# Turned copies, squares, values and distances on ScalarE, normalisation on GpSimd, and attention seams reordered, in a fused decoder layer on one core

## The chip, the core and the metric

The kernel runs on one core of a Trainium2 chip. The metric is the device time of one execution in microseconds; of the kernel before there are three runs, 987.98, 996.69 and 997.89 us, median 996.69 us. The engines are TensorE (PE, with its weight loads as PEld), VectorE (DVE), ScalarE (ACT), GpSimd (POOL) and SyncE (SP), which here only issues DMAs. Each engine takes its own instructions in order, and they wait for one another through semaphores.

## The reference, cut to what matters

The input x has 4 batches of 1024 rows of 256; the context has 4 x 77 rows of 256. All arithmetic is float32.

```
xn = layernorm(x)                                  # "x" normals
q, k, v = xn @ Wq / 4, xn @ Wk, xn @ Wv            # 16 heads of 16
A = (q k^T)^2, causal;  o = (A v) / (sum A + 1e-5) # per head
x1 = x + o @ Wo                                    # "wo"
s = layernorm(x1)                                  # "student" normals
D = sqrt(max(|ctx|^2 + |s|^2 - 2 ctx s^T, 0))      # 77 x 1024, "dist"
path = backtrack(dtw(D))                           # "warp": forward, backward
x2 = x1 + path^T @ ctx                             # "along"
y = layernorm(x2)                                  # "ffn" normals
out = x2 + gelu(y @ W1' + b') @ W2' + bias         # "hidden", "out"
```

W1' and W2' are W_exp and W_con multiplied by ten butterfly stages each; the kernel folds these once ("coef", "chain", "up", "mix", "w1", "down").

## The kernel before

One written list of units, `make_plan` (L94), sets the order of everything. Every engine's program loops over the same list (L567 GpSimd, L589 ScalarE, L775 VectorE, L988 TensorE, and the DMA queue of SyncE at L381) and does its part of each unit, so the relative order of all work on each engine is that of the list. `woven(parts, fill)` spreads a list of fill units evenly behind the parts.

- **Attention** of a batch is 48 steps (`attention_steps`): four groups of four heads, two halves of 512 query columns, key tiles of 128. A step n issues scores of n+1 on PE into `psS` (pair a, then b), products of n-1 into `psO`; ScalarE squares the scores into `A` (L609); GpSimd masks the diagonal tiles (L564); VectorE finishes a half (`heads_out`, L681). The first score of a batch waits for `s_stack`: the q and k parts are split into three bfloat16 pieces (L600 on ScalarE, L835 to L840 on VectorE), stored to HBM and read back stacked by twelve DMAs (`parts_out` L397, `stack_in` L404).
- **psW items.** All other matmul results go through the two banks of `psW` in turn. PE waits for `s_free` of the item two before; the reader waits for `s_ready`.
- **A layer norm** is `norm_units` (L68): four "stats" units of two 128x256 tiles (VectorE L800), "variance" (VectorE L805, L808, then ScalarE takes the root, L593), "rstd" (VectorE waits for the root, L811), four "normal" units of two tiles (VectorE L816), which write XN. Then four "turn" items: PE transposes four tiles into a bank (L1012) and VectorE copies it out (L825).
- **front(b)** is the norm of x, the turns, and eight "qk" items (PE L1021). **back(b)** is the student norm, then for each half of the 1024 columns two turns, whose squares ScalarE makes from the SBUF copy (L615), and one "dist" item: PE multiplies the context and the copy (L1049) and, after `s_sqt`, ones and the squares (L1052); VectorE adds and clips (L858), ScalarE takes the root (L623), SP stores (L418, L420). **values(b)** are four items (PE L1028, VectorE L844), **wo(b)** four (PE L1041, VectorE L853 adds to X).
- **Warps.** Two batches are warped together on VectorE: 104 forward rows (L730, L731, L733), whose distances SP reads back (L468), and 104 backward rows (L751, L752, L754). Each row depends on the one before. Warp 0 is woven with attention of batches 2 and 3, warp 1 with the feed-forward of batches 0 and 1. `ready(b)` adds along (L1102, L853), takes the ffn norm and turns; "hidden" is PE L1112 and a gelu on ScalarE (L655); "out" is PE L1122 and VectorE L940, L946.
- **Seams.** Behind the last steps of batch b the list has `values(b + 1) + both(b + 1) + wo(b)`, `both` being the first two scores. ready(0) is woven into the last four steps of batch 3, and back(3) into hidden(0, 0).
- **GpSimd's program** begins with constants, then for b = 1 to 3 waits for X of batch b-1 to land and issues the load of batch b (L537), then makes seven WIDEN tiles (L540); after that it enters the list.

## Time and profile before

| | |
|---|---|
| median of three runs | 996.69 us |
| the profiled execution, its own time | 998.89 us |
| its span, first to last instruction | 997.1 us |
| busy: PE, PEld | 795.2 us (80%), 385.3 us (39%) |
| busy: DVE, ACT, POOL | 603.5 us (61%), 405.9 us (41%), 124.6 us (12%) |
| mean granted TensorE clock | 0.883 |
| chain that ended last | DVE 33%, PE 25%, DMA 6% of the span |

Busy shares are means over stretches with different limits; the rows further down give them by stretch. PE lines are L966 (scores), L983 (products), L1028 (values), and so on as above. In a row of the trace, "xN" is a count, and the brackets at its end say how long the engine had been idle before it and what ended that. A timeline merges like instructions that follow each other on one engine. A granted clock of 1.00 is 2.4 GHz.

### The profile page before, as it was taken

The numbers are of one execution on the slowest core, as the hardware profiler recorded it, in microseconds if no ns is written. First come the engines' busy times: TensorE is split into PE (matmuls) and PEld (weight loads), VectorE is DVE, ScalarE is ACT, GpSimd is POOL, SyncE is SP. The second block draws the span as 40 slices with busy tenths as digits, with TensorE's granted clock in tenths as the row PEclk, the third lists the DMA queues.
The fourth block names the chain that finished last, engine by engine and source line by source line (L and its number), as shares of the span: only waits on it lengthen the run. The fifth ranks groups of instructions, "written<-read, shape, count | busy, mean of one in ns | idle before, by whom it ended". The sixth has DMA issues, their size and how long they took to land.

```text
span 997.1 us, 12566 instructions
## 1 busy us (share of the span) xinstructions
PE 795.2 (80%) x3919; PEld 385.3 (39%) x3919; DVE 603.5 (61%) x2611; ACT 405.9 (41%) x578; POOL 124.6 (12%) x306
## 2 busy tenths in 40 slices
PE   4889899998899897897777587796799342299998
PEld 2434234442234431233411122543575232256757
DVE  5743556433566427998599974646799888524002
ACT  1157874566673566652265555053013000032130
POOL 2123321132121122211121221000000000000000
PEclk9989899998799998898796798598799766599999
DMA  9785507665306753317505502001010001100001
GB/s 298 173 135 65 64 1 129 125 72 72 40 1 125 130 69 47 47 66 138 63 16 63 72 9 37 7 1 22 13 37 20 9 22 43 31 1 10 33 1 42
DMA packets 52133, 58.56 MB, mean 59 GB/s; under 512 B 22631, under 2 KB 31819, under 8 KB 52067
## 3 DMA queue, kind: packets, MB, share of 16 engines
q1 hardware_dynamic: 50979, 53.57, 31.5%
q0 software_dynamic: 1088, 4.19, 1.5%
q8 instruction: 31, 0.51, 0.2%
q14 instruction: 35, 0.29, 0.1%
HBM read 36.24 MB, written 21.50 MB: 58 GB/s over the span
## 4 chain that ended last, share of the span: by engine, by line
DVE 33%; PE 25%; DMA 6%; issue 3%; ACT 1%; SPq 1%; DVEq 0%; ACTq 0%
PE psS L1112 7%; PE psW L1122 6%; DVE FOLD L733 6%; DVE FOLD L754 6%; DVE FOLD L731 3%; DVE FOLD L752 3%; PE psW L1041 2%; DVE FOLD L730 2%; DVE FOLD L751 2%; DMA dist<-ARENA 2%; PE psS L966 2%; PE psW L1102 2%; PE psO L983 2%; DMA MORE<-dist 1%; DVE XX L816 1%
## 5 line engine op out<-in xcount | busy, mean ns | idle before, releaser
L609 ACT ACTIVATE ARENA<-psS 128x1024 f32<-128x1024 f32 (+3 forms) x384 | 295.1, 808 | 168.8 <-PE psS L966 165.7
L966 PE MATMUL psS<-ARENA 96*128 96x512 bf16 (+3 forms) x768 | 195.1, 351 | 62.5 <-ACT ARENA L609 54.9
L983 PE MATMUL psO<-ARENA 128*32 128x512 f32 (+3 forms) x1536 | 176.7, 535 | 1.5 <-POOL ARENA L564 1.5
L564 POOL TENSOR_SCALAR_AFFINE_SELECT ARENA<-ARENA 128x256 f32<-128x256 f32 x256 | 109.4, 433 | 469.7 <-ACT ARENA L609 466.9
L966 PEld LDWEIGHTS psS<-ARENA 96*128 96x128 bf16 x768 | 54.8, 101 | 250.1 <-ACT ARENA L609 180.5
L1122 PE MATMUL psW<-W2E,ARENA 128*128 128x256 f32 x512 | 116.2, 388 | 31.3 <-DVE ARENA L946 31.3
L1122 PEld LDWEIGHTS psW<-W2E,ARENA 128*128 128x128 f32 x512 | 99.3, 195 | 48.3 <-DVE ARENA L946 32.6
L655 ACT ACTIVATE ARENA<-psS,BEFF 128x512 f32<-128x512 f32 x64 | 43.4, 687 | 144.8 <-PE psS L1112 144.7
L1021 PE MATMUL psW<-XX,ARENA 128*128 128x512 f32 x128 | 63.3, 629 | 7.0 <-DVE XX L825 3.9
L1012 PE MATMUL psW<-IDENT,XX 128*128 128x128 f32 x192 | 34.8, 327 | 39.6 <-DVE XX L816 32.0
L754 DVE TENSOR_TENSOR_SCAN FOLD<-FOLD 64x37 bf16<-64x37 bf16 x208 | 61.8, 297 | 7.3
L733 DVE TENSOR_TENSOR_SCAN FOLD<-FOLD,MORE 64x37 f32<-64x37 f32 x208 | 60.8, 292 | 7.3
L853 DVE TENSOR_TENSOR X<-X,psW 128x512 f32<-128x512 f32 x32 | 21.9, 686 | 68.8 <-PE psW L1102 44.0
L593 ACT ACTIVATE SD<-VE 128x8 f32<-128x8 f32 x12 | 2.5, 206 | 141.8 <-DVE VE L808 141.8
L1112 PE MATMUL psS<-XX,MIXA 128*128 128x512 f32 x128 | 59.0, 607 | 0.0
L983 PEld LDWEIGHTS psO<-ARENA 128*32 128x32 f32 x1536 | 31.5, 112 | 69.1 <-issue 49.6
L1112 PE MATMUL psS<-ARENA,MIXA 128*128 128x512 f32 x128 | 55.3, 592 | 0.0
L730 DVE TENSOR_TENSOR FOLD<-FOLD 64x37 f32<-64x37 f32 x208 | 40.3, 194 | 15.5 <-DMA MORE<-dist 11.1
L1102 PE MATMUL psW<-CTX,ARENA 77*128 77x256 f32 x64 | 21.1, 486 | 34.0 <-DMA ARENA<-path 34.0
L1012 PEld LDWEIGHTS psW<-IDENT,XX 128*128 128x128 f32 x192 | 27.6, 169 | 50.2 <-issue 38.1
L1028 PE MATMUL psW<-ARENA,XX 128*128 128x256 f32 x128 | 35.2, 439 | 12.4 <-DVE ARENA L844 7.9
L751 DVE TENSOR_TENSOR FOLD<-FOLD 64x37 bf16<-64x37 bf16 x206 | 37.7, 183 | 5.8
(115 smaller groups left out, 793.1 us busy)
## 6 DMA issues: line engine op xcount, KB each, us to landing
ARENA<-qk_parts SPq DMA_DIRECT2D x192, 128.0 KB, 7.1
qk_parts<-ARENA SPq DMA_DIRECT2D x16, 768.0 KB, 4.3
out<-ARENA SPq DMA_DIRECT2D x16, 256.0 KB, 2.2
X<-in_x POOLq DMA_DIRECT2D x3, 1024.0 KB, 9.7
dist<-ARENA SPq DMA_DIRECT2D x4, 425.0 KB, 10.7
MORE<-dist SPq DMA_DIRECT2D x32, 52.6 KB
path<-MORE SPq DMA_DIRECT2D x52, 32.4 KB
dist<-ARENA SPq DMA_DIRECT2D x4, 300.5 KB
```

The costliest lines, as they stand in the source:

```text
L564: pool.affine_select(out=blk, in_=blk, compare_op=ALU.is_ge, fill=0.0, base=0, pattern=[[0, 2], [1, P]], channel_multiplier=-1).then_inc(s ...
L609: nc.scalar.activation(A[:, (2 * G + a) % A_PAIRS, :, 0:N], psS[:, a, :, 0:N], ACT.Square).then_inc(s_sq, 1)
L730: nc.vector.tensor_tensor(out=least, in0=above[:, 1:CB + 1], in1=above[:, 0:CB], op=ALU.min).then_inc(s_pre, 1)
L733: nc.vector.tensor_tensor_scan(row[:, 1:CB + 1], least, DSK[:, t // CH % 2, t % CH], row[:, 0:1], ALU.min, ALU.add).then_inc(s_row, 1)
L751: nc.vector.tensor_tensor(out=two, in0=below[:, 0:CB], in1=below[:, 1:CB + 1], op=ALU.add).then_inc(s_enter, 1)
L754: nc.vector.tensor_tensor_scan(row[:, 0:CB][:, ::-1], KIND[:, t][:, ::-1], two[:, ::-1], row[:, CB:CB + 1], ALU.subtract, ALU.is_lt).then_ ...
L966: ins = nc.tensor.matmul(psS[:, a, j, 0:N], KST[0:STACK, g % 2, 2 * a + j, kt * P:(kt + 1) * P], QST[0:STACK, g % 2, 2 * a + j, q0:q0 + N] ...
L983: ins = nc.tensor.matmul(psO[32 * j:32 * j + 32, o % 2, q0 - qc * HALF:q0 - qc * HALF + N], V1[:, kt, GH * g + j], A[:, (2 * G + j // 2) % ...
L1012: ins = nc.tensor.transpose(W[:, t * P:(t + 1) * P], XN[:, 4 * h + t, k * P:(k + 1) * P], IDENT[:])
L1021: ins = nc.tensor.matmul(W, WQKV[:, k, s * D + m * P:s * D + (m + 1) * P], XNT[:, k, h * HALF:(h + 1) * HALF], start=k == 0, stop=k == KD - 1)
L1112: ins = nc.tensor.matmul(psS[:, (n % 4) // 2, n % 2], W1E[:, k, m * P:(m + 1) * P], XFT[b % 2][:, k, h * HALF:(h + 1) * HALF], start=k == ...
L1122: ins = nc.tensor.matmul(W[:, j * D:(j + 1) * D], HGE[:, h, m, c:c + P], W2E[:, m, 0:D], start=m == 0, stop=m == HT - 1)
```

## The change

- The copies of "value", "turn_s" (student) and "turn_f" (ffn) items, and the add and clip of "dist", go from VectorE to ScalarE, which reads the PSUM bank itself; the squares of turned student tiles are made from PSUM too, and the bank is freed behind them. `s_sqt` goes; the "dist" matmuls wait for the turns' `s_free` alone. "turn_x" copies stay on VectorE.
- "normal" units go from VectorE to GpSimd. It waits for a new semaphore `s_rstd`, and for the last turn of the norm before.
- ScalarE's root becomes a unit of its own, "root", and empty "pause" units stand between variance, root and rstd.
- In the list, `both(b + 1)` comes before the last products of batch b and before values(b + 1) (in batch 0 too); wo(b) is woven into the statistics of back(b) of the next batch. back(3) and then ready(0) stand alone, in order, behind batch 3; warp 1 starts behind them, woven with both halves of hidden of batch 0.

```diff
@@ -65,13 +65,15 @@
...
 
-def norm_units(kind, b, before=()):
+def norm_units(kind, b, before=(), gap=0):
 
...
         stats = list(before[:2]) + sum(([s, u] for s, u in zip(stats, before[2:])), []) + stats[len(before) - 2:]
-    return stats + [("variance", kind, b), ("rstd", kind, b)] + [("normal", kind, b, i) for i in range(TT // 2)]
+    pause = [("pause",)] * gap
+    return (stats + [("variance", kind, b)] + pause + [("root", kind, b)] + pause + [("rstd", kind, b)]
+            + [("normal", kind, b, i) for i in range(TT // 2)])
 
...
@@ -94,11 +96,11 @@
...
     ns = len(attention_steps())
-    front = lambda b: norm_units("x", b) + [("turn_x", b, i) for i in range(4)] + [("qk", b, i) for i in range(8)]
-
-    def back(b, before=()):
+    front = lambda b, gap=2: norm_units("x", b, (), gap) + [("turn_x", b, i) for i in range(4)] + [("qk", b, i) for i in range(8)]
+
+    def back(b, gap=2):
         halves = [[("turn_s", b, 2 * h), ("turn_s", b, 2 * h + 1), ("dist", b, h)] for h in range(2)]
-        return norm_units("student", b, before) + sum(halves, [])
+        return norm_units("student", b, wo(b), gap) + sum(halves, [])
     values = lambda b: [("value", b, i) for i in range(TT // 2)]
...
@@ -120,27 +122,28 @@
...
 
-    plan = front(0) + [("w_exp", i) for i in range(4)] + values(0) + both(0)
+    plan = front(0, 0) + [("w_exp", i) for i in range(4)] + both(0) + values(0)
     for b, fill in ((0, [("context", i) for i in range(B)] + up + front(1)), (1, back(0) + down + front(2))):
         steps = steps_of(b)
-        plan += steps[0] + flat(woven(steps[1:-3], fill)) + flat(steps[-3:]) + values(b + 1) + both(b + 1) + wo(b)
+        plan += steps[0] + flat(woven(steps[1:-3], fill)) + flat(steps[-3:-1]) + both(b + 1) + steps[-1] + values(b + 1)
 
     steps = steps_of(2)
-    third = woven(steps[:LEAD], back(1)) + woven(steps[LEAD:-3], front(3)) + steps[-3:] + [values(3) + both(3) + wo(2)]
+    third = (woven(steps[:LEAD], back(1, 1)) + woven(steps[LEAD:-2], front(3)) + [steps[-2] + both(3)] + steps[-1:]
+             + singles(values(3)))
     steps = steps_of(3)
     fourth = woven(steps[:-LAST], back(2))
-    plan += flat(third[:LEAD + SLACK]) + flat(woven(third[LEAD + SLACK:] + fourth, warp(0))) + paths(0)
-    plan += flat(steps[-LAST:-4]) + flat(woven(steps[-4:], ready(0)))
-
-    plan += wo(3)[:2] + flat(woven(singles(back(3, wo(3))[2:]), hidden(0, 0)))
-    rest = [hidden(0, 1), ready(1), outs(0, 0) + outs(0, 1), hidden(1, 0) + hidden(1, 1), outs(1, 0) + outs(1, 1)]
-    pieces = woven(singles(rest[0]), rest[1]) + singles(rest[2] + rest[3] + rest[4])
+    plan += flat(third[:LEAD + SLACK]) + flat(woven(third[LEAD + SLACK:] + fourth, warp(0))) + paths(0) + flat(steps[-LAST:])
+
+    plan += back(3, 0) + ready(0)
+    rest = [hidden(0, 0) + hidden(0, 1), ready(1), outs(0, 0) + outs(0, 1), hidden(1, 0) + hidden(1, 1), outs(1, 0) + outs(1, 1)]
+    pieces = singles(rest[0][:HT]) + woven(singles(rest[0][HT:]), rest[1]) + singles(rest[2] + rest[3] + rest[4])
     plan += flat(woven(pieces, warp(1), [4 if piece[0][0] == "out" else 1 for piece in pieces])) + paths(1) + ready(2)
...
 
+ON_SCALAR = ("qk", "value", "turn_s", "turn_f", "dist")
 ITEM_KINDS = ("context", "w_exp", "turn_x", "qk", "value", "wo", "turn_s", "dist", "coef", "chain", "up", "w1", "down", "along", "turn_f", "out")
...
@@ -568,6 +572,15 @@
...
                     mask(*u[1:])
+                elif kind == "normal":
+                    _, what, b, i = u
+                    if i == 0:
+                        pool.wait_ge(s_rstd, norm_of[what, b] + 1)
+                        if norm_of[what, b]:
+                            pool.wait_ge(s_ready, ready(*turned[norm_of[what, b] - 1]))
+                    for t in (2 * i, 2 * i + 1):
+                        ins = pool.tensor_scalar(XN[:, t], X[:, b, t], MV[:, t, 0:1], RS[:, t:t + 1], ALU.subtract, ALU.mult)
+                    ins.then_inc(s_xn, 1)
                 elif kind == "coef" and u[1] == 1:
...
@@ -588,7 +601,7 @@
...
                 kind = u[0]
-                if kind == "variance":
+                if kind == "root":
                     act.wait_ge(s_var, norm_of[u[1:]] + 1)
...
@@ -607,19 +620,36 @@
...
                     nc.scalar.activation(A[:, (2 * G + a) % A_PAIRS, :, 0:N], psS[:, a, :, 0:N], ACT.Square).then_inc(s_sq, 1)
+                elif kind == "value":
+                    _, b, i = u
+                    act.wait_ge(s_ready, ready(*u))
+                    for j in range(2):
+                        ins = nc.scalar.activation(V1[:, 2 * i + j, :, 0:HD],
+                                                   psW[:, bank(*u), j * D:(j + 1) * D].rearrange("p (h e) -> p h e", h=NH), ACT.Copy)
+                    ins.then_inc(s_free[bank(*u)], 1)
                 elif kind == "turn_s":
...
                     h, k = i // 2, i % 2
-                    act.wait_ge(s_free[bank(*u)], made(*u))
+                    if i == 0 and b + 1 < B:
+                        act.wait_ge(s_parts_out, 64 * (b + 2))
+                    act.wait_ge(s_ready, ready(*u))
                     SNT, SQT = BACK[b][0:2]
-                    nc.scalar.activation(SQT[:, k, h * HALF:(h + 1) * HALF], SNT[:, k, h * HALF:(h + 1) * HALF],
-                                         ACT.Square).then_inc(s_sqt, 1)
+                    nc.scalar.activation(SNT[:, k, h * HALF:(h + 1) * HALF], psW[:, bank(*u)], ACT.Copy)
+                    nc.scalar.activation(SQT[:, k, h * HALF:(h + 1) * HALF], psW[:, bank(*u)], ACT.Square).then_inc(s_free[bank(*u)], 1)
+                elif kind == "turn_f":
+                    _, b, i = u
+                    h, k = i // 2, i % 2
+                    act.wait_ge(s_ready, ready(*u))
+                    nc.scalar.activation(XFT[b % 2][:, k, h * HALF:(h + 1) * HALF], psW[:, bank(*u)], ACT.Copy).then_inc(s_free[bank(*u)], 1)
                 elif kind == "dist":
...
                         act.wait_ge(s_dist_out[B - 2], 32)
+                    act.wait_ge(s_ready, ready(*u))
+                    DSQ, DN = BACK[b][2:4]
+                    nc.scalar.activation(DSQ[0:S, h * HALF:(h + 1) * HALF], psW[0:S, bank(*u)], ACT.Relu, bias=AA[:, b:b + 1]
+                                         ).then_inc(s_free[bank(*u)], 1)
                     act.wait_ge(s_free[bank(*u)], made(*u))
-                    DSQ, DN = BACK[b][2:4]
                     nc.scalar.activation(DN[0:S, h * HALF:(h + 1) * HALF], DSQ[0:S, h * HALF:(h + 1) * HALF],
...
@@ -801,6 +831,8 @@
...
                     settled()
+                    if norm_of[u[1:]]:
+                        dve.wait_ge(s_xn, TT // 2 * norm_of[u[1:]])
                     for t in range(TT):
...
@@ -808,21 +840,13 @@
...
                     dve.wait_ge(s_sd, norm_of[u[1:]] + 1)
-                    vec(nc.vector.reciprocal(RS[:], SD[:]))
-                    settled()
-                elif kind == "normal":
-                    _, what, b, i = u
-                    for t in (2 * i, 2 * i + 1):
-                        ins = nc.vector.tensor_scalar(XN[:, t], X[:, b, t], MV[:, t, 0:1], RS[:, t:t + 1],
-                                                      ALU.subtract, ALU.mult)
-                    ins.then_inc(s_xn, 1)
-                elif kind in ("turn_x", "turn_s", "turn_f"):
+                    nc.vector.reciprocal(RS[:], SD[:]).then_inc(s_rstd, 1)
+                elif kind == "turn_x":
                     _, b, i = u
                     h, k = i // 2, i % 2
-                    if kind == "turn_s" and i == 0 and b + 1 < B:
-                        dve.wait_ge(s_parts_out, 64 * (b + 2))
-                    dst = {"turn_x": XNT, "turn_s": BACK[b][0], "turn_f": XFT[b % 2]}[kind]
-                    nc.vector.tensor_copy(dst[:, k, h * HALF:(h + 1) * HALF], got).then_inc(freed, 1)
+                    if b and i == 0:
+                        dve.wait_ge(s_ready, ready("value", b - 1, TT // 2 - 1))
+                    nc.vector.tensor_copy(XNT[:, k, h * HALF:(h + 1) * HALF], got).then_inc(freed, 1)
                 elif kind == "qk":
...
@@ -852,11 +870,6 @@
...
                                             op=ALU.add).then_inc(freed, 1)
-                elif kind == "dist":
-                    _, b, h = u
-                    DSQ = BACK[b][2]
-                    nc.vector.tensor_scalar(DSQ[0:S, h * HALF:(h + 1) * HALF], got[0:S], AA[:, b:b + 1], 0.0,
-                                            ALU.add, ALU.max).then_inc(freed, 1)
                 elif kind == "w1":
```

## Rows read from the trace of the kernel before

**Rows 1.** Windows of five stretches: busy us (count), granted clock, DMA share, GB/s.

```profile
186.00:317.00 131.00, 117.76 (x695) 41.79 (x694) 65.31 (x158) 87.74 (x133) 28.72 (x71) 0.92 0.41 59
384.00:612.00 228.00, 170.10 (x966) 59.27 (x970) 192.77 (x1023) 111.91 (x155) 40.72 (x94) 0.83 0.36 56
612.00:684.00 72.00, 63.09 (x245) 33.20 (x238) 31.19 (x86) 29.64 (x39) 3.25 (x8) 0.86 0.16 19
...
719.00:856.00 137.00, 78.76 (x287) 55.36 (x285) 123.53 (x782) 12.28 (x17) 0.00 (x0) 0.80 0.08 25
856.00:997.00 141.00, 126.78 (x448) 85.57 (x448) 33.63 (x78) 26.03 (x37) 0.00 (x0) 0.92 0.07 20
```

**Rows 2.** Timeline of POOL, first 42 us: start, duration, operation, idle before.

```profile
27.30 0.88 POOL L537 DMA_DIRECT2D X<-in_x  x1 [9.10 <-DMA X<-in_x]
28.18 2.48 POOL L540 COPY FOLD<-IDENT 64x128 f32<-64x128 f32 x7
```

**Rows 3.** Timeline of DVE over the first 42 us.

```profile
10.50 2.67 DVE L816 TENSOR_SCALAR XX<-X,MV,RS 128x256 f32<-128x256 f32 x8
```

**Rows 4.** Timeline of PE over the first 75 us.

```profile
18.14 17.93 PE L1021 MATMUL psW<-XX,ARENA 128*128 128x512 f32 x32 [2.27 <-DMA WOP<-in_L_attn_Wo]
...
41.72 8.27 PE L1028 MATMUL psW<-ARENA,XX 128*128 128x256 f32 x32
53.69 1.41 PE L966 MATMUL psS<-ARENA 96*128 96x512 bf16 x4 [3.70 <-DMA ARENA<-qk_parts]
```

**Rows 5.** Timeline of the SP queue over the first 75 us.

```profile
38.43 11.11 SPq L411 DMA_DIRECT2D ARENA<-qk_parts  x24
```

**Rows 6.** Timeline from 300 to 345 us, the seam of batches 1 and 2.

```profile
304.76 0.60 ACT L600 ACTIVATE ARENA<-psW 128x512 bf16<-128x512 f32 x1 [0.69 <-PE psW L1021]
...
315.93 0.64 PE L983 MATMUL psO<-ARENA 128*32 128x256 f32 x8
...
317.40 7.25 PE L1028 MATMUL psW<-ARENA,XX 128*128 128x256 f32 x32
...
326.41 1.06 PE L966 MATMUL psS<-ARENA 96*128 96x512 bf16 x4 [1.76 <-DMA ARENA<-qk_parts]
...
327.28 8.76 PE L1041 MATMUL psW<-WOP,ARENA 128*128 128x256 f32 x32
```

**Rows 7.** Groups of DVE, 384 to 612 us: busy, mean ns, idle before, releaser.

```profile
L754 DVE TENSOR_TENSOR_SCAN FOLD<-FOLD 64x37 bf16<-64x37 bf16 x104 | 32.0, 308 | 3.7
...
L816 DVE TENSOR_SCALAR XX<-X,MV,RS 128x256 f32<-128x256 f32 x16 | 5.8, 400 | 0.0
...
L844 DVE COPY ARENA<-psW 128x256 f32<-128x256 f32 x8 | 2.9, 409 | 4.5 <-PE psW L1028 4.5
...
L853 DVE TENSOR_TENSOR X<-X,psW 128x512 f32<-128x512 f32 x4 | 2.7, 686 | 5.0 <-PE psW L1041 5.0
...
L825 DVE COPY ARENA<-psW 128x512 f32<-128x512 f32 x4 | 2.7, 664 | 0.8 <-PE psW L1012 0.8
...
L858 DVE TENSOR_SCALAR ARENA<-psW,AA 77x512 f32<-77x512 f32 x2 | 1.5, 748 | 7.0 <-PE psW L1052 7.0
```

**Rows 8.** Groups of POOL from 384 to 612 us.

```profile
L564 POOL TENSOR_SCALAR_AFFINE_SELECT ARENA<-ARENA 128x256 f32<-128x256 f32 x94 | 40.7, 439 | 178.1 <-ACT ARENA L609 176.9
```

**Rows 9.** Groups of DVE from 719 to 856 us.

```profile
L754 DVE TENSOR_TENSOR_SCAN FOLD<-FOLD 64x37 bf16<-64x37 bf16 x104 | 29.7, 286 | 3.7
```

**Rows 10.** The chain that ended last, by time: start, us, what.

```profile
661.49 1.72 PE psW L1049 x4
...
674.55 7.16 DMA dist<-ARENA
```

**Rows 11.** Timeline of DVE from 682 to 722 us.

```profile
684.13 0.19 DVE L730 TENSOR_TENSOR FOLD<-FOLD 64x37 f32<-64x37 f32 x1 [5.19 <-DMA MORE<-dist]
...
697.57 0.17 DVE L811 RECIPROCAL RS<-SD 128x8 f32<-128x8 f32 x1
...
718.66 2.29 DVE L940 TENSOR_TENSOR ARENA<-X,BIAS 128x2048 f32<-128x2048 f32 x1 [4.78 <-PE psW L1122]
```

More of the change, by code:

```diff
@@ L160, in layer @@
     item_of = {u: k for k, u in enumerate(u for u in plan if u[0] in ITEM_KINDS)}
+    turned = [u for u in plan if u[0] in ("turn_x", "turn_s", "turn_f") and u[2] == 3]
     norm_of = {u[1:3]: k for k, u in enumerate(u for u in plan if u[0] == "variance")}
@@ L309, in layer @@
         s_sd = sem("s_sd")
+        s_rstd = sem("s_rstd")
         s_xn = sem("s_xn")
```

10 lines of the change are left out of this document (1 added, 9 removed).

## The prediction

> **What bounds the kernel now.** I read the windows first, then the chain of waits and the engine timelines at each joint, then the groups of VectorE. The span has four kinds of stretch. Up to the first score at 53.69 us everything is serial: statistics, normalisation, turning, q and k, a round trip of q/k parts through HBM, scores [rows 3 to 5]. Then three attention batches run near TensorE's limit: 117.8 of 131 us busy, at a granted clock of 0.92 [rows 1]. From 384 to 612 us the first warp is woven in and VectorE bounds: 192.8 of 228 us busy against 170.1 on PE and 111.9 on ACT, and what is missing is mostly VectorE waiting inside its own order (7.0 us for distances, 5.0 for wo, 4.5 for values) [rows 1, 7]. From 719 to 856 us VectorE's second warp bounds alone (123.5 of 137 us), and from 856 us PE does (126.8 of 141) [rows 1]. So an instruction taken off VectorE is worth its length in two stretches and nothing where PE bounds; and a step moved in the serial head costs all its delay.
>
> **Start: normals go behind GpSimd's loads.** Now the normals of batch 0 begin at 10.50 us on DVE [rows 3]. In the new program they stand in GpSimd's order after its three loads of X, each issued only when the one before has landed, and after the seven WIDEN copies: the last issue is at 27.30 us, the copies end at 30.66 [rows 2]. Nothing in the diff moves these. The wait is 30.66 - 10.50 = 20.2 us. No row shows a tensor_scalar on GpSimd. Nearest is its affine_select of the same 128x256 tile, 439 ns [rows 8]; below it zero is the end, above it the WIDEN copies, 2.48/7 = 0.35 us for half as many columns, so 0.71 us [rows 2]. I take 0.44: eight make 3.5 us against DVE's 2.67, +0.8. Of this, 1.5 us is forgiven, since the q matmuls wait 2.27 us for weights now [rows 4]. The last X load overlapped the first stores of q/k and no longer does, my estimate is -3 us (0 to -4). The first score comes 16.5 us later, near 70 us. Second, the values: 8.27 us of PE at 41.72, done today under the wait for the stacked parts (which take from 38.43 to 53.69) [rows 4, 5]. The new plan puts them after the first scores, in the open: +8.3, less 1.8 for squares that now lie beside them. **Start: +23** (17 to 29).
>
> **Two seams, 0 to 1 and 1 to 2.** The fourth q/k piece is ready at 304.76 us, the stack has landed at 326.41: 21.6 us. The last-but-one products end at 316.57, and the values fill 317.40 to 324.65, so PE waits 1.76 us only [rows 6]. The new order asks for the next batch's first scores right after the last-but-one products. The pieces before it are the same, so PE stands from 316.6 to 326.4, and then does last products (0.4) and values (7.25). Step 1 starts at about 326.4 + 1.1 + 0.6 + 7.3 + 1.5 (slower clock after a stop, an estimate: the first 128x256 values at 41.72 took 8.27 against 7.25 here) = 336.9, against 336.0 today (327.28 + 8.76) [rows 4, 6]. Today wo lies inside that time, in the new plan its 32 matmuls, of the shape of the values, 7.3 us, are still to come, woven into steps where PE is already 90% busy [rows 1]. I take 5 of them as not hidden (0 to 7.3). **Seams: 2 x 6 = +12** (-4 to +17). ScalarE takes the values here: eight copies, shorter than the 0.60 us of a 128x512 one [rows 6], beside 7.25 us of PE: nothing; their cover is gone only if ScalarE becomes full. The third seam costs nothing: VectorE is behind there.
>
> **384 to 612 us.** Off VectorE go 16 normals (5.8 us), 8 value copies (2.9), 4 turned copies (2.7), 2 distances (1.5): 12.9 us. With them go the waits in which it stood for the distance matmuls (7.0), values (4.5), turns (0.8), and, as wo is spread, 4 of 5.0 [rows 7]: 16.3 us. GpSimd costs something back: the warp's scan takes 308 ns here and 286 where GpSimd rests [rows 7, 9], 2.3 us over 104; with the warp's three like instructions some 7 us beside 40.7 us of GpSimd [rows 8]; 16 normals add 7 us of it, so +1.2 to 2. Next late are the DMAs of distance rows and ACT: it gets 8 value copies, 4 turned copies at 0.60 and 2 relus, 8 us on 111.9 of 228 [rows 1, 6], covered. The pauses let VectorE reach rstd after the root is done, and ACT the root after the variance. Pool's masks queue behind normals that wait for rstd; products wait for masks, but PE is ahead of VectorE. **-27** (-10 to -32).
>
> **612 to 719 us.** Today 72.1 us pass from the end of warp 0 to the first row of warp 1, 684.13 [rows 1, 11], with ready(0) and half of the hidden layer before it. New: rest of attention 12 us, wo 7, last add, statistics and variance 4, root, rstd and four normals 2, then two turns, four ScalarE passes (0.60 each [rows 6]), two pairs of distance matmuls (2 x 1.72 each [rows 10]), relu and root, for two halves: 17; the store and first load of distances as today, 674.19 to 684.13, 10 [rows 10, 11]. That is 52, and ready(0) fits under the DMA. Warp 1 starts 20 us earlier. Normals and turned copies of ready(1) also leave VectorE (-5), but it now reaches the first out product, 21 us behind rstd today (697.57 to 718.66), with more wait than today's 4.78 us, about 8, because 16 hidden tiles come later (+3), and four pieces done before 684 fall behind the start (+3) [rows 11]. **-19** (-9 to -23). The cover of the new order is the DMA's 10 us; without it ready(0) would be in the open.
>
> **Tail.** ready(2) and ready(3) gain 8 and 4 normals on the way, 0.1 us each, and copies that queue behind gelus: **+1** (0 to +4) on the 141 us [rows 1]. That ScalarE squares from PSUM rather than SBUF I cost at nothing; it was busy beside the same matmuls before.
>
> Sum: 23 + 12 - 27 - 19 + 1 = **-10 us**, from the profiled 998.89 (span 997.1) to 989. That execution lies 2.2 above the median of 996.69, and its changes are taken over: 987; I say **988**.
>
> **A rule against the change.** GpSimd's same-sized select takes 439 ns and DVE's normal 400 [rows 7, 8], hardly different. The Trainium skill, GPSIMD Engine Reference, section 4.1, calls GpSimd about 2x slower than VectorE for two-input elementwise work, though one-input is "roughly line-rate". By the first half of it a normal would take 0.8 us, and as 28 of them lie on the path the sum would be 998; by that page's second half it stays 988.
>
> **Rivals.** (a) *The seams are free*: the stack lands earlier, since its contending store is later, and wo hides under squares: seams -2 instead of +12, warp stretch at its full 30: 971. For it: ACT has 43 us free in 186 to 317 [rows 1]; against: 21.6 us from the fourth piece is a chain of two DMAs [rows 6]. Chance 0.25. (b) *GpSimd's normals are dear*, the case on the other side: some 28 normals stand alone in a chain (8 at the start, 4 in back(3), 4 in ready(1), 12 in the tail), plus the blocked warp instructions, 30 us of time per us of normal. It decides slower than before from (997 - 988)/30 + 0.44 = 0.74 us each, and over 1% slower from 1.06; at 1.2 us the time is 1011. For it: 0.35 us for half a tile in WIDEN; against: 439 ns [rows 2, 8]. Chance 0.18. (c) *Another engine holds the 384 to 612 stretch*: GpSimd waits for rstd, masks wait, PE (170.1 of 228 busy) catches up too late, and only 10 of 27 us come: 1005. For it: PE's granted 0.83 [rows 1]; against: VectorE has no wait for products there. Chance 0.17. My forecast 0.40. That the copies don't move isn't possible; the code names the engine.
>
> **Numbers.** What a measurement of this kernel can tell from no change is 1%, 986.7 to 1006.7. My forecast itself spans 978 to 999 and gives 0.17 faster, 0.23 same; (a) 0.23 and 0.02; (b) 0.15 slower, 0.03 same; (c) 0.10 same, 0.07 slower. Together 0.40, 0.38, 0.22. Range 965 to 1012: it leaves out the far ends of (a) and (b).
>
> **What would show it.** In the profile after: first normal on GpSimd at 30.7 us and first score near 70; a PE wait of 7 to 10 us for the stacked parts at both seams; the warp stretch about 200 us long with no DVE wait for distances; first row of warp 1 about 52 us after warp 0; normals of 0.4 to 0.5 us. Wrong if normals start before 25 us, if they take over 0.8, or if the first stretch's loss is given back in batch 0.

## The result and the profile after

| kernel | median, us | runs, us | against before |
|---|---|---|---|
| before | 996.71 | 987.98 to 997.89 | |
| changed | 1043.26 | 1041.46 to 1046.35 | 1.049 [1.0426, 1.0555] |

The changed kernel is 4.9% slower. The forecast was 988 us with a range to 1012, so sign and range are both missed. The profiled execution of the changed kernel took 1041.46 us (span 1039.7).

The groups of the changed kernel's page, by cost (columns as in [rows 7]):

```profile
L568 POOL TENSOR_SCALAR_AFFINE_SELECT ARENA<-ARENA 128x256 f32<-128x256 f32 x256 | 107.7, 427 | 415.7 <-ACT ARENA L622 413.2
L582 POOL TENSOR_SCALAR XX<-X,MV,RS 128x256 f32<-128x256 f32 x96 | 118.1, 1241 | 257.5 <-DVE RS L843 257.5
L1025 PE MATMUL psW<-IDENT,XX 128*128 128x128 f32 x192 | 38.1, 350 | 96.1 <-POOL XX L582 93.7
L979 PE MATMUL psS<-ARENA 96*128 96x512 bf16 (+3 forms) x768 | 193.7, 348 | 59.0 <-DMA ARENA<-qk_parts 35.9
```

One number stands out. A normal takes 1241 ns on GpSimd. The forecast took 440, from the select in the first row, which is still as quick as in [rows 8]. TensorE's turns stand idle for 93.7 us in all behind those normals, against 38.0 us behind VectorE's in kernel a below. The last row is the seams: 35.9 us of waiting for stacked parts.

The start, on POOL and then on PE (start us, duration, operation, idle before), answers to [rows 2 to 4]:

```profile
26.90 0.88 POOL L541 DMA_DIRECT2D X<-in_x  x1 [8.27 <-DMA X<-in_x]
27.77 1.69 POOL L544 COPY FOLD<-IDENT 64x128 f32<-64x128 f32 x7
29.47 9.64 POOL L582 TENSOR_SCALAR XX<-X,MV,RS 128x256 f32<-128x256 f32 x8
```

```profile
34.45 1.94 PE L1025 MATMUL psW<-IDENT,XX 128*128 128x128 f32 x8 [34.45 <-POOL XX L582]
39.26 1.94 PE L1025 MATMUL psW<-IDENT,XX 128*128 128x128 f32 x8 [2.87 <-POOL XX L582]
42.03 17.64 PE L1034 MATMUL psW<-XX,ARENA 128*128 128x512 f32 x32 [0.83 <-issue]
73.91 1.89 PE L979 MATMUL psS<-ARENA 96*128 96x512 bf16 x4 [8.42 <-DMA ARENA<-qk_parts]
```

The queue is as forecast: loads, WIDEN, then normals at 29.47 us. But eight of them last 9.64 us and not 3.5, and the first score comes at 73.91 us, 20.2 later than in [rows 4].

The seam of batches 1 and 2 (from the last products of one batch to the first scores of the next) in the changed kernel, PE, answers to [rows 6]:

```profile
370.01 0.64 PE L996 MATMUL psO<-ARENA 128*32 128x256 f32 x8
380.61 1.89 PE L979 MATMUL psS<-ARENA 96*128 96x512 bf16 x4 [9.96 <-DMA ARENA<-qk_parts]
383.01 8.27 PE L1041 MATMUL psW<-ARENA,XX 128*128 128x256 f32 x32
```

The scores are asked for before the values, so PE stands for 9.96 us. Before, the values filled that time and left 1.76. At the seam of batches 0 and 1 it is 7.61 us, so both lie in the 7 to 10 that the forecast named.

To see where time is lost I read the same events in each trace: the first scores of each batch, the last products, and the first and last row of warp 1. This table gives the length between them, to about half a microsecond, since a row is taken by its start. Kernels j, a, o and c are experiments below; j copies where the others normalise, so its results are not those of the layer.

| stretch, us | before | changed | j: 0.4 us copies in place of the normals, GpSimd | a: normals on VectorE | o: half of them | c: best |
|---|---|---|---|---|---|---|
| to first score | 53.7 | 73.9 | 65.7 | 51.3 | 53.6 | 53.4 |
| batch 0 | 122.8 | 137.4 | 129.9 | 132.6 | 137.8 | 124.9 |
| batch 1 | 150.0 | 169.3 | 157.3 | 155.9 | 168.7 | 148.3 |
| batch 2 | 159.2 | 156.1 | 152.6 | 152.8 | 158.0 | 146.1 |
| batch 3 | 146.4 | 122.8 | 121.4 | 121.3 | 124.1 | 118.9 |
| to first row of warp 1 | 52.2 | 42.4 | 39.3 | 40.0 | 39.7 | 39.8 |
| warp 1 | 170.0 | 181.2 | 169.7 | 171.4 | 171.5 | 171.5 |
| from its last row to the end | 142.9 | 156.6 | 144.7 | 144.6 | 143.9 | 144.5 |
| span | 997.1 | 1039.7 | 980.6 | 969.8 | 997.2 | 947.3 |

### The profile page after: what moved, and what is told of

The parts are those of the page before. It is cut to its first block, busy times and chain, and to the rows that moved or that the text cites. A ratio compares the mean times of both kernels' runs of the same rounds, so it can differ in the third digit from the quotient of the medians.

```text
span 1039.7 us, 12584 instructions
## 1 busy us (share of the span) xinstructions
PE 794.4 (76%) x3919; PEld 385.5 (37%) x3919; DVE 537.2 (52%) x2443; ACT 431.0 (41%) x644; POOL 239.6 (23%) x402
## 4 chain that ended last, share of the span: by engine, by line
PE 39%; DVE 27%; POOL 8%; issue 8%; DMA 8%; ACT 6%; SPq 2%; POOLq 0%; DVEq 0%; ACTq 0%
POOL XX L582 7%; PE psS L979 7%; PE psO L996 7%; PE psW L1134 6%; DVE FOLD L784 5%; PE psS L1124 5%; DVE FOLD L763 4%; DMA ARENA<-qk_parts 4%; ACT ARENA L622 3%; PE psW L1041 2%; DMA X<-in_x 2%; DVE FOLD L782 2%; DVE FOLD L761 2%; PE psW L1054 2%; PE psW L1034 2%
## 5 line engine op out<-in xcount | busy, mean ns | idle before, releaser
L979 PE MATMUL psS<-ARENA 96*128 96x512 bf16 (+3 forms) x768 | 193.7, 348 | 59.0 <-DMA ARENA<-qk_parts 35.9
L996 PE MATMUL psO<-ARENA 128*32 128x512 f32 (+3 forms) x1536 | 174.4, 528 | 15.3 <-POOL ARENA L568 14.9
L582 POOL TENSOR_SCALAR XX<-X,MV,RS 128x256 f32<-128x256 f32 x96 | 118.1, 1241 | 257.5 <-DVE RS L843 257.5
L1134 PE MATMUL psW<-W2E,ARENA 128*128 128x256 f32 x512 | 114.6, 385 | 20.5 <-DVE ARENA L959 20.2
L1025 PE MATMUL psW<-IDENT,XX 128*128 128x128 f32 x192 | 38.1, 350 | 96.1 <-POOL XX L582 93.7
L1025 PEld LDWEIGHTS psW<-IDENT,XX 128*128 128x128 f32 x192 | 30.2, 184 | 109.0 <-issue 105.1
L718 DVE STREAM_TRANSPOSE ARENA<-psO 128x512 f32<-128x512 f32 x32 | 22.5, 704 | 77.9 <-PE psO L996 77.8
L1124 PE MATMUL psS<-XX,MIXA 128*128 128x512 f32 x128 | 62.2, 640 | 0.0
L1124 PE MATMUL psS<-ARENA,MIXA 128*128 128x512 f32 x128 | 55.3, 592 | 0.0
L613 ACT ACTIVATE ARENA<-psW 128x512 bf16<-128x512 f32 x32 | 19.1, 597 | 75.6 <-PE psW L1034 75.6
L760 DVE TENSOR_TENSOR FOLD<-FOLD 64x37 f32<-64x37 f32 x208 | 42.7, 206 | 7.7 <-DMA MORE<-dist 2.5
## 6 DMA issues: line engine op xcount, KB each, us to landing
dist<-ARENA SPq DMA_DIRECT2D x4, 425.0 KB, 10.5
```

Source lines behind the costliest of these rows:

```text
L582: ins = pool.tensor_scalar(XN[:, t], X[:, b, t], MV[:, t, 0:1], RS[:, t:t + 1], ALU.subtract, ALU.mult)
L979: ins = nc.tensor.matmul(psS[:, a, j, 0:N], KST[0:STACK, g % 2, 2 * a + j, kt * P:(kt + 1) * P], QST[0:STACK, g % 2, 2 * a + j, q0:q0 + N] ...
L996: ins = nc.tensor.matmul(psO[32 * j:32 * j + 32, o % 2, q0 - qc * HALF:q0 - qc * HALF + N], V1[:, kt, GH * g + j], A[:, (2 * G + j // 2) % ...
L1025: ins = nc.tensor.transpose(W[:, t * P:(t + 1) * P], XN[:, 4 * h + t, k * P:(k + 1) * P], IDENT[:])
L1124: ins = nc.tensor.matmul(psS[:, (n % 4) // 2, n % 2], W1E[:, k, m * P:(m + 1) * P], XFT[b % 2][:, k, h * HALF:(h + 1) * HALF], start=k == ...
L1134: ins = nc.tensor.matmul(W[:, j * D:(j + 1) * D], HGE[:, h, m, c:c + P], W2E[:, m, 0:D], start=m == 0, stop=m == HT - 1)
```

## The experiments

Each was timed beside the kernel before on the same chip. The experiments lie on four chips, on which the kernel before had medians of 995.5 to 998.5 us, so a difference of 2 or 3 us between kernels of two chips may be the chip's. My theory after the result (G) was that GpSimd's price of a normal costs nearly all; the rivals were the new order at the seams (S) and VectorE's stretch taking back what is given (C).

### a: all normals on VectorE

```
-                elif kind == "normal":                       # GpSimd
-                        ins = pool.tensor_scalar(XN[:, t], ...)
+                elif kind == "normal":                       # VectorE, waits s_rstd
+                        ins = nc.vector.tensor_scalar(XN[:, t], ...)
```

> The changed kernel with all 96 normals back on VectorE; the plan, the ScalarE part and the seams stay as changed. Theory G (the normals on GpSimd are what makes the changed kernel slow: 1241 ns each there instead of 400 on VectorE, 8 of them behind the X loads in the start): first score back from 73.9 to about 53 us, the 8 normals of a chain back from 9.6 to 3.4 us, so 980 to 1000 us, 43 to 60 below the changed kernel. Theory S (the new order at the seams and in the start is what costs): no more than 25 us come back, 1018 us or more. Theory C (VectorE then holds the stretch of warp 0 as in the kernel before, and what the start gives back is lost there): about 1005 us, with the stretch of warp 0 some 15 us longer than in the changed kernel.

Measured: 970.89 us (969.9 to 971.6), 0.9743 [0.9702, 0.9784] of before. 72 us come back, more than G expected; S and C are out as the main cause (c shows below that the order costs too). Without its GpSimd part the change is a gain of 2.6%. Against the changed kernel the table gives 22.6 us in the start, 18.2 in batches 0 and 1, 4.8 in batches 2 and 3, 2.4 to the first row, 9.8 in warp 1, 12.0 in the tail: 69.8 of 69.9.

### e: only the normals moved

```
 (kernel before)
-                        ins = nc.vector.tensor_scalar(XN[:, t], ...)
+                        ins = pool.tensor_scalar(XN[:, t], ...)
```

> The kernel before with nothing changed but the engine of the 96 normals, which is GpSimd. Theory G: about 1240 ns each, the start 20 us later, 6 us more in each of the chains that PE waits for (student 3, ffn 0 to 3) and masks held back in batches 0 and 1: 1035 to 1055 us. Theory S: the normals cost only the start, 1010 to 1018 us.

Measured: 1045.57 us, 1.0504 [1.0451, 1.0557]. As G expected. This one move alone costs 47 us (1045.6 - 998.5), as much as the whole change. It costs more still in the new order, 72 us by a. Against before, the profiled execution of e loses 20.3 us in the start, 12.5 in batches 0 and 1, 8.2 on the way to warp 1 and 13.0 in the tail. In the new order batches 0 and 1 lose 18.2 and warp 1 another 9.8, where e loses nothing. Why the new order feels the normals more there, no run sets apart.

### d: only the ScalarE part, in the order of before

```
 (changed kernel, normals on VectorE)
-    make_plan() as changed
+    make_plan() as before, "root" put between "variance" and "rstd"
```

> The kernel before, its order of work as it was, with only the ScalarE part of the change: value copies, copies and squares of turned tiles, and distances read from PSUM on ScalarE; the normals stay on VectorE. Theory G: VectorE loses about 31 us of copies (32 turns and 32 value pairs and 8 distances) while it holds the stretch of warp 0, so 975 to 990 us. Rival (ScalarE, which squares every pair of scores, holds batches 0 to 2 when it copies too, and PE's values wait for it): 997 to 1005 us, with PE waiting for psW behind ScalarE at each values block.

Measured: 978.69 us, 0.9822 [0.9771, 0.9873]. As G expected. Warp 0 lasts 211.9 us instead of 229.2. ScalarE hardly holds anything: PE's waits for it before scores are 29.1 us in all, against 54.9 before, and new are 10.1 us before the distance matmuls, which now wait for ScalarE's copies.

### f: what makes a normal dear

```
+            pool.wait_ge(s_ready, ready("turn_f", 3, 3))
+            for r in range(3):
+                pool.tensor_scalar(XN[:, 0], X[:, 3, 0], MV[:, 0, 0:1], RS[:, 0:1], ALU.subtract, ALU.mult)
+                pool.tensor_scalar(XN[:, 1], X[:, 3, 1], 0.5, 2.0, ALU.subtract, ALU.mult)
+                pool.tensor_scalar(XN[:, 2], X[:, 3, 2], MV[:, 2, 0:1], None, ALU.subtract)
+                pool.tensor_scalar(XN[:, 3], X[:, 3, 3], 0.5, None, ALU.subtract)
+                pool.tensor_copy(XN[:, 4], X[:, 3, 4])
+                pool.tensor_tensor(out=XN[:, 5], in0=X[:, 3, 5], in1=X[:, 2, 5], op=ALU.mult)
+                pool.tensor_scalar(XN[:, 6:8], X[:, 3, 6:8], MV[:, 6, 0:1], RS[:, 6:7], ...)
```

> The first of these kernels (normals on VectorE) with 21 extra GpSimd instructions once the last tiles are turned, in three rounds, on unused space, 128x256 each: the normal as it is (two values per partition), the same with two constants, a subtraction alone with a value per partition, the same with a constant, a copy, a product of two tensors, and one normal over 128x512. Theory 1 (the two per-partition values make it dear): 1.2 us for the first and about 0.4 to 0.5 us for those with constants or one operation. Theory 2 (GpSimd takes that long for any fp32 tile of this size, each operation adding): copy and one operation about 0.6 us, two operations about 1.2 us whatever their scalars. Theory 3 (it is fixed cost): the 128x512 one takes hardly more than the 128x256 one.

One run (975.13 us). Groups of POOL from 900 us on, where the last round and a part of the second lie (busy us, mean ns):

```profile
L616 POOL TENSOR_SCALAR XX<-X,MV,RS 128x512 f32<-128x512 f32 x2 | 4.2, 2078 | 0.0
L613 POOL TENSOR_SCALAR XX<-X 128x256 f32<-128x256 f32 x2 | 1.7, 847 | 0.0
L615 POOL TENSOR_TENSOR XX<-X 128x256 f32<-128x256 f32 x2 | 1.5, 729 | 0.0
L610 POOL TENSOR_SCALAR XX<-X,MV,RS 128x256 f32<-128x256 f32 x1 | 1.2, 1222 | 0.1
L611 POOL TENSOR_SCALAR XX<-X 128x256 f32<-128x256 f32 x1 | 1.1, 1071 | 0.0
L612 POOL TENSOR_SCALAR XX<-X,MV 128x256 f32<-128x256 f32 x1 | 0.9, 922 | 0.0
L614 POOL COPY XX<-X 128x256 f32<-128x256 f32 x2 | 0.8, 396 | 0.0
```

None of the three theories fits whole; the second is nearest. A copy is 396 ns. One operation with a constant is already 847, a second adds 224 (1071 - 847), two values per partition instead of constants 151 (1222 - 1071). It is not fixed cost: twice the columns take 2078 - 1222 = 856 ns more. So the price follows the operation. Copy and select are the cheap ones, and besides memsets they are all that GpSimd computed in the trace of before, the select at this size and the copies at smaller ones.

These rows leave out the normal of the second round. It took 3.13 us, and it began beside a VectorE add whose two inputs both lie in SBUF (POOL, then DVE):

```profile
894.42 3.13 POOL L610 TENSOR_SCALAR XX<-X,MV,RS 128x256 f32<-128x256 f32 x1
```

```profile
894.16 2.29 DVE L982 TENSOR_TENSOR ARENA<-X,BIAS 128x2048 f32<-128x2048 f32 x1 [10.19 <-PE psW L1163]
```

The normals of the first and third rounds took 1227 and 1222 ns. So GpSimd seems to have been held up for 1.9 us by VectorE (one case, no run sets it apart), but that isn't what makes the 96 normals dear. In the changed kernel the shortest takes 1208 ns, the median 1218 and the longest 1579.

### b: the start alone cured

```
+def on_pool(what, b):
+    return (what, b) != ("x", 0)
-                elif kind == "normal":                       # GpSimd
+                elif kind == "normal" and on_pool(*u[1:3]):  # GpSimd; else VectorE
```

> The changed kernel with the 8 normals of x of batch 0 alone on VectorE; the other 88 stay on GpSimd. It divides the cost of the start from that of the rest. Theory Q (what counts is the queue: the first normals stand behind the three loads of X and the widening on GpSimd): the start gives back 22 us (73.9 to about 51 us at the first score), and of the 72 us between the changed kernel and the one with all normals on VectorE most of the rest, about 50, stays: 1018 to 1024 us. Theory W (the start hides the later waits, so that curing it helps little): 1032 us or more.

Measured: 1023.56 us, 1.0256 [1.024, 1.0271]. Theory Q in its size; whether the queue or the price holds the start, m divides. The start gives 20 us (1043.3 - 1023.6), and 53 stay in the other 88 normals (1023.6 - 970.9).

### m: the loads behind the normals

```
-            for b in range(1, B): ... pool.dma_start(X[:, b], ...)      # ahead of the plan
+                    if (what, b, i) == ("x", 0, TT // 2 - 1):
+                        loads_and_widen()
```

> The changed kernel, its normals on GpSimd, with the three loads of X for batches 1 to 3 and the ten widening copies issued on GpSimd behind the normals of batch 0 instead of ahead of them. The 20 us that the first score came later are divided so: about 14 for standing in the queue, about 6 for eight instructions of 1.24 us. So: first score at about 60 us, and 1043 less 14 = 1027 to 1031 us. Rival: if the X loads then collide with the stacked parts of batch 0, the first score stays above 65 us and the time above 1034.

Measured: 1028.03 us, 1.0328 [1.0289, 1.0366]. First score at 56.8 us, 3 earlier than expected. The widening copies that moved with the loads are seven, as in [rows 2], not ten. The 22.6 us between the first scores of the changed kernel and of a divide into 17.1 of queue (73.9 - 56.8) and 5.5 of dearer normals (56.8 - 51.3). The normals themselves start 18.9 us earlier (10.60 against 29.47). The missing 1.8 us lie between the first q and k matmul and the first score, 33.7 us against 31.9: with loads of X under way, the parts are stored and asked back in 10.1 us instead of 7.5. So the loads seem to hold the parts up, but by little.

### j: the forecast's own premise

```
-                        ins = pool.tensor_scalar(XN[:, t], X[:, b, t], MV[:, t, 0:1], RS[:, t:t + 1], ALU.subtract, ALU.mult)
+                        ins = pool.tensor_copy(XN[:, t], X[:, b, t])
```

> The changed kernel with GpSimd copying X into the place of the normalised tiles instead of normalising it, same size, same queue, same waits; the division by the spread and the subtraction of the mean are left out, statistics and everything else stay. A copy of 128x256 took 393 ns on GpSimd, a normal 1241 ns. So this is the changed kernel as the forecast had it, with a 0.4 us normal, still behind the X loads. Theory P (the forecast's error is the price of a normal and nothing else): 985 to 993 us, that is the forecast's 988 or the 970.9 of the kernel with VectorE's normals and some 18 us of queue in the start. Theory Q (a good part comes from where the normals stand in GpSimd's queue, between the masks and behind the loads, whatever they cost): 1005 us or more.

Measured: 984.93 us (982.29 to 987.05), 0.9896 [0.9866, 0.9926]. Its groups of POOL:

```profile
L568 POOL TENSOR_SCALAR_AFFINE_SELECT ARENA<-ARENA 128x256 f32<-128x256 f32 x256 | 108.1, 428 | 432.4 <-ACT ARENA L622 429.1
L582 POOL COPY XX<-X 128x256 f32<-128x256 f32 x96 | 34.8, 408 | 263.8 <-DVE RS L843 263.8
```

Theory P. The kernel leaves out the subtraction and the multiplication. With 408 ns in the place of each normal, same queue and waits, the change is worth -10.5 us (984.93 against 995.46), where the forecast had -9. What moves the time to 1043 is 0.83 us more for each of 96 instructions.

### o: which normals count

```
+def on_pool(what, b):
+    return (what == "x" and b > 0) or (what == "student" and b < 3)
```

> The changed kernel with its normals divided by the forecast's own list: those of x 0, student 3 and ffn 0 to 3 (48, among them all that the forecast held to be in a chain) on VectorE; those of x 1 to 3 and student 0 to 2 (48, all beside attention, held to cost 1 to 2 us of slowed VectorE and nothing else) on GpSimd at 1241 ns. Theory L (the forecast's list is complete; it only undercounted within it): 971 to 976 us, the time of the kernel with all normals on VectorE. Theory M (the batches that TensorE bounds lose too, for PE stands in one order behind each late turn and each late mask, and runs at a lower granted clock after it; the two traces differ by 18 us in batches 0 and 1 and by 5 in batches 2 and 3): 988 to 996 us.

Measured: 997.97 us (995.26 to 1000.01), 1.0013 [0.9994, 1.0032]. Theory M, and 2 us past its range. The 48 normals that the forecast priced at 1 to 2 us cost 27 (998.0 - 970.9). By the table they lose 18.0 us in batches 0 and 1, 5.2 in batch 2, 2.8 in batch 3, and 2.3 ahead of the first score.

How a normal beside attention reaches TensorE is in the timeline of POOL late in batch 0 of the changed kernel:

```profile
160.73 1.30 POOL L568 TENSOR_SCALAR_AFFINE_SELECT ARENA<-ARENA 128x256 f32<-128x256 f32 x3 [0.76 <-ACT ARENA L622]
162.02 2.42 POOL L582 TENSOR_SCALAR XX<-X,MV,RS 128x256 f32<-128x256 f32 x2
164.41 0.76 POOL L568 TENSOR_SCALAR_AFFINE_SELECT ARENA<-ARENA 128x256 f32<-128x256 f32 x2
165.16 5.07 POOL L582 TENSOR_SCALAR XX<-X,MV,RS 128x256 f32<-128x256 f32 x4
170.19 0.76 POOL L568 TENSOR_SCALAR_AFFINE_SELECT ARENA<-ARENA 128x256 f32<-128x256 f32 x2
```

and on PE, in the same window:

```profile
167.97 0.63 PE L1025 MATMUL psW<-IDENT,XX 128*128 128x128 f32 x4 [1.31 <-POOL XX L582]
171.09 1.51 PE L996 MATMUL psO<-ARENA 128*32 128x384 f32 x8 [2.38 <-POOL ARENA L568]
```

The masks that the products need stand behind a pair of normals of 2.4 us, and turns stand in PE's one order ahead of scores. The waits of PE over batches 0 and 1, for the changed kernel and then for j (us in all, times, longest):

```profile
PE psW L1025 <- POOL XX L582: 8.5, 4, 4.1
PE psO L996 <- POOL ARENA L568: 2.4, 1, 2.4
```

```profile
PE psW L1025 <- POOL XX L582: 0.7, 1, 0.7
```

That is 10.2 us of the 19.5 by which these two batches differ. Windows of them give the rest, in the same order (columns of [rows 1]):

```profile
74.00:211.00 137.00, 118.23 (x719) 45.99 (x719) 56.65 (x146) 89.58 (x137) 40.80 (x88) 0.92 0.45 70
211.00:381.00 170.00, 139.10 (x777) 57.21 (x778) 62.21 (x148) 96.84 (x150) 48.30 (x89) 0.88 0.41 66
```

```profile
66.00:196.00 130.00, 115.03 (x721) 44.79 (x720) 56.70 (x146) 89.59 (x137) 33.94 (x88) 0.95 0.48 76
196.00:353.00 157.00, 132.79 (x777) 55.20 (x776) 62.35 (x148) 96.57 (x150) 34.78 (x89) 0.90 0.43 69
```

The same matmuls are busy 257.3 us and 247.8 us: 9.5 more, at a granted clock of 0.92 and 0.88 instead of 0.95 and 0.90. So the loss is about twice the waits. It isn't an accident of one execution: over these two batches PE is busy 256.6 to 257.3 us in the four kernels of the new order with GpSimd's normals there (changed, o, b, m), and 246.2 to 250.3 in all nine others with ScalarE's copies (250.3 is a). But standing as such isn't the cause either. In j and a PE stands 26.0 and 28.3 us for stacked parts around these batches, in c at most 4.0, and it is busy 248.0, 250.3 and 247.7 us. Why PE is slower beside GpSimd's normals stays open.

### c: seams and start in the order of before

```
-        plan += ... flat(steps[-3:-1]) + both(b + 1) + steps[-1] + values(b + 1)
+        plan += ... flat(steps[-3:]) + values(b + 1) + both(b + 1)
 (the same for values(0) + both(0) and for values(3) + both(3); normals on VectorE)
```

> All normals on VectorE, and the start and the three seams between batches in the order of the kernel before (last products, then values, then the first scores of the next batch); the output projection of a batch stays inside the next piece, and all behind attention stays as changed. Theory O (the new order at the seams costs: PE waits 38 us in five places for stacked parts in the run with VectorE's normals, 3 us in the one with the order of before): 955 to 964 us against 970.9, with batch 2 starting near 322 us instead of 339.7. Rival R (whatever the seams give comes back off warp 0, whose rows VectorE must do anyway): 968 us or more, with the end of attention again near 614 us.

Measured: 947.14 us (942.72 to 949.05), 0.9483 [0.9457, 0.9509]. It is the fastest here, faster than both kernels, and by 8 us faster than I expected: batches 0, 1 and 2 each give 7 to 8 us (7.7, 7.6, 6.7) and batch 3 2.4, while the first score, now behind the values, comes 2.1 later. PE's waits for stacked parts, over the four batches' starts, in a and then in c:

```profile
PE psS L996 <- DMA ARENA<-qk_parts: 35.8, 4, 11.4
```

```profile
PE psS L995 <- DMA ARENA<-qk_parts: 4.0, 2, 2.3
```

### g: only the start and two seams

```
-    third = ... woven(steps[LEAD:-3], front(3)) + steps[-3:] + [values(3) + both(3)]
+    third = ... woven(steps[LEAD:-2], front(3)) + [steps[-2] + both(3)] + steps[-1:] + singles(values(3))
 (c otherwise; this line is the changed kernel's)
```

> As the one before it, but only the start and the first two seams have the order of before; the seam from batch 2 to 3, inside which warp 0 is woven, stays as changed. Theory O: 950 to 960 us, the first two seams being worth about 17 us and the third nothing or little. Rival R: 968 us or more, as above. If the third seam matters too, this one is some 5 us slower than the one with all seams as before.

Measured: 951.85 us, 0.9532 [0.9517, 0.9548]. Inside O's range, but the third seam counts too: 4.7 us against c. The forecast had said that it costs nothing because VectorE is behind there.

### h: GpSimd only where VectorE bounds

```
+def on_pool(what, b):
+    return (what, b) in (("x", 3), ("student", 1), ("student", 2))
 (g otherwise)
```

> As the one before it (start and first two seams in the order of before), but the normals of student 1, of x 3 and of student 2, all three in the stretch in which VectorE does the rows of warp 0, on GpSimd: 24 of 96. Theory B (VectorE holds this stretch, so 9.6 us of work taken off it are gained even at three times the price on an engine that is free there): 4 to 9 us faster than its sibling. Theory K (the chain of a normal is longer by 6 us each time and the masks stand behind it on GpSimd, and VectorE's own instructions slow down beside it): 3 to 15 us slower than its sibling.

Measured: 956.61 us, 0.9582 [0.9565, 0.9599], 4.8 slower than g: theory K at its low end. But not all 24 stand in the stretch that VectorE bounds. Those of student 1 run from 348 to 359 us, ahead of warp 0 and on the way to its distances, and its first row comes 4.6 us later (384.6 against 380.0). The other 16 do help VectorE: warp 0 is 2.6 us shorter. The way from it to warp 1 is then 3.2 longer, so they gain nothing in the end. VectorE's row instructions in warp 0 are slowed by 1.7 us in all (137.0 against 135.3); the backward scan takes 308 ns in both, the forward one 308 against 300. PE waits for GpSimd, in this stretch:

```profile
PE psO L1013 <- POOL ARENA L575: 12.2, 4, 8.8
PE psW L1042 <- POOL XX L589: 4.3, 2, 3.0
```

Not all of that is lost. In g the turns wait 14.5 us for VectorE's normals, here 10.5 for those and 4.3 for GpSimd's. The products wait 4.9 us in g and 12.4 here. All waits of PE together are 55.3 and 59.8 us.

### i: ready(0) back inside attention

```
-    plan += ... + flat(steps[-LAST:])
-    plan += back(3, 0) + ready(0)
+    plan += ... + flat(steps[-LAST:-4])
+    plan += flat(woven(steps[-4:], ready(0)))
+    plan += back(3, 0)
 (c otherwise)
```

> The best kernel so far (VectorE's normals, seams of before, 947.1 us) with one thing put back as it was in the kernel before: the units that add the aligned rows of batch 0, normalise and turn it (ready 0) stand inside the last four steps of attention, not behind the distances of batch 3. Theory T (PE then waits inside attention for the path of warp 0 to come back from memory, and the student norm of batch 3 starts that much later): 960 to 968 us, with the last products near 608 instead of 591.5 us. Rival U (it costs attention, but the first feed-forward tiles are ready earlier and give it back): 945 to 953 us.

Measured: 970.55 us, 0.9758 [0.9728, 0.9788]. Theory T, 2.6 us past its range. Batch 3 is 12.2 us longer and the way to warp 1 10.2. On PE among the last steps:

```profile
591.53 5.46 PE L1131 MATMUL psW<-CTX,ARENA 77*128 77x256 f32 x12 [5.75 <-DMA ARENA<-path]
```

PE waits for the path of warp 0 with two steps of attention behind it, and warp 1 later waits for the distances of batch 3. This order is 23.4 of the 31.5 us between d and c, and the largest single gain that these runs set apart.

### n: x turns on ScalarE too

```
+                elif kind == "turn_x" and u[1]:              # ScalarE
+                    nc.scalar.activation(XNT[...], psW[:, bank(*u)], ACT.Copy)
```

> The best kernel so far, with the copies of turned x tiles of batches 1 to 3 moved to ScalarE too (12 of 16, 0.69 us each on VectorE). Theory B (VectorE holds the stretch of warp 0): the four of batch 3 give 1 to 3 us there, nothing elsewhere: 943 to 947 us. Rival (ScalarE stands behind its squares, so the turned tiles come later and the parts of q and k with them): 948 to 955 us, the waits for stacked parts longer.

Measured: 947.33 us, 0.9518 [0.949, 0.9545]: the same as c within what can be measured. Neither the gain nor the loss.

## Why the prediction was wrong

The forecast gave each part a number. The table sets them beside what changed from before, first in j, where the forecast's price of a normal holds, and then in the changed kernel.

| part, us | forecast | j | changed |
|---|---|---|---|
| up to the first row of warp 0 (start and two seams) | +35 | +34.2 | +63.9 |
| warp 0 | -27 | -25.2 | -23.3 |
| from its last row to the first of warp 1 | -19 | -27.0 | -22.9 |
| warp 1 | in the -19 | -0.3 | +11.2 |
| tail | +1 | +1.8 | +13.7 |
| sum | -10 | -16.5 | +42.6 |

(j's timed gain is 10.5 us; its profiled execution was a quick one and that of before is above its median.)

**The step that failed is "I take 0.44".** It took the price of a normal from the select of the same tile [rows 8], kept 0.71 us as its upper end, and the chip needs 1.24. No row of the trace of before had a GpSimd arithmetic operation. The select and the copies of [rows 2] were neighbours by their tiles and not by kind, and so neither was a bound. The text even said what would make it wrong, "if they take over 0.8".

**A second step was mis-sized: the slope.** Rival (b) named the right mechanism and the right side, with chance 0.18, and gave 1011 us at 1.2. It counted 28 normals in a chain, 30 us per us. From j to the changed kernel 58.3 us come for 0.83 us, 70 per us. Part of it is the count: the start, the way to warp 1, warp 1 and the tail, where all of the 28 stand, lose 34.7 us by the table (8.2 + 3.1 + 11.5 + 11.9), where 28 times 0.83 is 23. The rest is in the four batches, 24.4 us, and o shows it from the other side: the 48 normals beside attention, costed at "+1.2 to 2", cost 27. The forecast asked whether VectorE or PE is bound there, but not what else stands in GpSimd's queue (masks) and in PE's (turns ahead of scores). Its sentence "masks queue behind normals that wait for rstd" was right and was waved off with PE being ahead of VectorE. It was written for the stretch of warp 0 alone; nothing was put down for batches 0 and 1, where PE bounds.

**The rule.** The normal takes 1241 ns on GpSimd and 400 on VectorE [rows 7], 3.1 times as long, with one tensor as input. The Trainium skill, GPSIMD Engine Reference, section 4.1, says about 2x slower for two-input work and roughly line-rate for one input. Its first half was nearer and still too kind. Its second half fits only the copy, 396 ns, and the select, 427. The price that the forecast worked out from the first half, 0.8 us, gave 998 us.

**The start** was right in its mechanism and dear in its sum. The queue was given 20.2 us less what is forgiven; m shows 18.9 for the queue, of which 17.1 reach the first score. In j, with the forecast's own price, the first score comes 12.0 us late and not 16.5. The -3 us for stores without a load of X beside them was an estimate that no row priced; from the first store of parts to the first read of them it is 11.4 us before and 7.5 in j, so 3.9. That this row of the table agrees so well, +34.2 for +35, is in part luck: the start was some 4 too high and the batches behind it as much too low. **The seams** were near in size (19.0 us from g to a, timed, for start values and two seams that were given 18.5) and wrong in their account. I had wo as the loss and the values as neutral; but c keeps wo spread and is rid of the loss, and d, with wo in its old place, spends 123.2 + 145.4 us in batches 0 and 1 against c's 124.9 + 148.3. So wo costs at most 2 or 3 us a batch, and what costs is PE standing for the parts with the values behind it, 7.6 or 7.7 us a batch. The third seam, "nothing", is 4.7 (g).

**Warp 0** was right: VectorE's waits for distances, values and wo are gone, and d shows that the ScalarE part alone makes it 17 us shorter. **612 to 719** was right and low: 50.5 us from warp to warp, 52 forecast, though with dear normals in it; i shows the order of ready(0) to be its main cause, 23.4 us. Of warp 1's 11.5 us over j, 7.1 are in these waits of VectorE, in the changed kernel and then in j:

```profile
DVE ARENA L953 <- PE psW L1134: 9.8, 1, 9.8
DVE X L871 <- PE psW L1114: 8.3, 2, 8.1
```

```profile
DVE ARENA L953 <- PE psW L1134: 5.7, 1, 5.7
DVE FOLD L760 <- DMA MORE<-dist: 2.9, 1, 2.9
DVE X L871 <- PE psW L1114: 2.4, 2, 2.2
```

ready(1)'s eight normals take 10.8 us there against 3.0 in j, and the first out product starts 12.6 us behind rstd against 8.3. **Tail:** the 16 normals of ready(2) and ready(3) hold PE directly, in the changed kernel's last stretch:

```profile
PE psW L1025 <- POOL XX L582: 15.4, 3, 8.5
```

I had costed 12 of them at 0.1 us each, which is the same wrong price again.

Rival (a), seams free, fell: with the start's order and the third seam they cost 24 us. Rival (c), that only 10 of the 27 us in warp 0 come, fell with the changed kernel itself: 23.3 came, dear normals and all.

## What to carry to other kernels

An operation's price on another engine is bounded only by a row of the same kind of operation there. If the trace has none, the bound is open, and a rival that turns the sign deserves far more than 0.18. A row of the same tile by another operation was off by 2.8 times here. Price a move by every queue that it enters: here each instruction stood between masks that one engine needed, and ahead of turns in another engine's single order. And a change of many parts may hold a gain of 5% under losses of 10%, so try the parts alone. Here the ScalarE part was worth 20 us and the order behind attention 23; the seams cost 24 and the normals on GpSimd 72.

## What the runs showed of the hardware

- GpSimd on a 128x256 float32 tile: copy 396 ns, select 427, product of two tensors 729, one operation with a constant 847, with a value per partition 922, two with constants 1071, two with values per partition 1222 to 1241. Two with values per partition on 128x512 take 2078. VectorE does the normal of 128x256 in 400 [rows 7].
- A GpSimd normal that began 0.26 us behind a 2.29 us VectorE add of two SBUF tensors took 3.13 us instead of 1.22 (f, one case).
- VectorE's backward scan in warp 0 takes 308 ns with GpSimd's normals beside it (h) and 308 without (g), the forward one 308 and 300. Over all row instructions of warp 0 it is 1.7 us, for 16 normals of 1.24 us. The forecast had 1.2 to 2 for 16 normals of 0.44.
- The same matmuls of batches 0 and 1 took 9.5 us more busy time where TensorE also waited 10.2 us more for GpSimd, at a granted clock of 0.92 and 0.88 instead of 0.95 and 0.90. With 26 to 28 us of standing at the seams instead (j and a against c) they took 0.3 and 2.6 us more.
